# Edge keys from products on 64 rows of the array, picked keys added by VectorE, and 3 picked tiles in 16 in place of 4

## The reference

```python
Q = (nodes @ wq + bq).reshape(n, H, DK)
K = (nodes @ wk + bk).reshape(n, H, DK)
V = (nodes @ wv + bv).reshape(n, H, DK)
scores = (Q[row] * K[col]).sum(-1) * inv_sqrt_dk
ef = (edge_attr @ we + be).reshape(-1, H, DK)      # edge_attr: 200000 x 64, we: 64 x 128
scores = scores + (Q[row] * ef).sum(-1) * inv_sqrt_dk
es = jnp.exp(scores)
denom = jax.ops.segment_sum(es, row, num_segments=n)
msg = (es / (denom[row] + 1e-08))[..., None] * V[col]
out = jax.ops.segment_sum(msg, row, num_segments=n).reshape(n, -1) @ wo + bo
```

## Time and profile before

| | |
|---|---|
| median of 3 runs (lowest to highest) | 4399.89 us (4384.28 to 4402.94) |
| the profiled execution, its time | 4383.41 us |
| its span | 4381.6 us |
| mean granted clock of TensorE | 0.96 of full speed |
| TensorE busy | 87% of the span |
| GpSimd busy | 66% |
| VectorE busy | 61% |
| ScalarE busy | 39% |

### The profile page before, as it was taken

The page is one execution under the profiler, slowest core; times in us unless marked ns, Lnnn a source line. Parts: engine busy times, 40 slices in busy tenths (PEclk is TensorE's granted clock), DMA queues, the critical chain, the costliest instruction groups (busy, mean ns, idle before and its releaser), DMA issues.

```text
span 4381.6 us, 91625 instructions
## 1 busy us (share of the span) xinstructions
PE 3832.3 (87%) x24957; PEld 2675.4 (61%) x24958; DVE 2673.1 (61%) x5858; ACT 1730.6 (39%) x4596; POOL 2880.5 (66%) x2878
## 2 busy tenths in 40 slices
PE   5557877369999999999995899999999999999994
PEld 3234444134454544545443688888888888888883
DVE  8999999231131311313115677777777777777777
ACT  0046666130010100101003566666666666666662
POOL 3167887777777777777776466666666666666660
PEclk8989999679999999999997999999999999999997
DMA  9525555479999899998993566666666666666661
GB/s 374 212 93 186 186 192 179 167 239 356 332 325 356 299 356 333 320 356 302 355 348 117 159 173 173 173 174 173 174 174 173 174 173 174 173 174 173 174 174 52
DMA packets 507359, 982.36 MB, mean 224 GB/s; under 512 B 280679, under 2 KB 298035, under 8 KB 505384
## 3 DMA queue, kind: packets, MB, share of 16 engines
q1 hardware_dynamic: 362280, 656.78, 45.9%
q0 software_dynamic: 113856, 229.87, 16.9%
q10 hardware_dynamic: 31168, 95.09, 6.5%
HBM read 781.05 MB, written 200.41 MB: 224 GB/s over the span
## 4 chain that ended last, share of the span: by engine, by line
PE 42%; POOL 37%; issue 12%; DVE 2%; ACT 1%; DMA 1%; DVEq 0%; SPq 0%; POOLq 0%; ACTq 0%
POOL records L1032 36%; PE ps L1805 10%; PE ps L1823 9%; PE ps L1809 8%; PE ps L1798 5%; PE ps L1815 4%; PE ps L1778 2%; PE ps L1776 2%; PE ps L1787 1%; PE ps L1438 1%; POOL recs L1014 0%; POOL recs L1015 0%; ACT deg L1481 0%; DVE deg L2141 0%; DVE st_f L2127 0%
## 5 line engine op out<-in xcount | busy, mean ns | idle before, releaser
L1032 POOL DMA_INDIRECT records<-recs,pos x1562 | 1619.9, 1037 | 478.9 <-issue 470.7
L1744 POOL DMA_INDIRECT kv<-kv_table,rec x1213 | 1168.3, 963 | 747.2 <-DVE msg L1989 423.0
L1154 PE MATMUL ps<-adj,mh 128*128 128x500 f16 (+1 forms) x6370 | 1309.0, 366 | 6.4 <-DVE mh L1305 5.6
L1154 PEld LDWEIGHTS ps<-adj,mh 128*128 128x128 f16 x6370 | 619.3, 97 | 675.1 <-issue 7.7
L1326 DVE TENSOR_TENSOR adj<-adj,quarter 128x128 f16<-128x128 f16 (+25 forms) x305 | 46.2, 210 | 766.1 <-DMA adj<-adj_full 758.2
L1809 PE MATMUL ps<-we,at 128*128 128x256 f32 x1616 | 483.0, 381 | 0.0
L1192 ACT ACTIVATE sc<-sc 128x1 f32<-128x1 f32 x6 | 1.2, 203 | 1216.0 <-DVE sc L1274 973.3
L1805 PE MATMUL ps<-qn,oht 128*128 x3232 | 457.1, 285 | 5.2 <-ACT at L1872 1.2
L1823 PE MATMUL ps<-msg,ohf 128*128 128x136 f32 x3232 | 443.0, 280 | 4.9 <-DVE msg L1989 4.9
L1805 PEld LDWEIGHTS ps<-qn,oht 128*128 128x128 f32 x3232 | 392.3, 191 | 75.9 <-issue 75.9
L866 ACT ACTIVATE blk<-ps 128x490 f16<-128x490 f32 x625 | 335.1, 587 | 226.9 <-PE ps L795 225.9
(11 more groups left out here) (325 smaller groups left out, 5378.0 us busy)
## 6 DMA issues: line engine op xcount, KB each, us to landing
adj<-adj_full SPq DMA_DIRECT2D x420, 875.0 KB, 6.0
x1t<-kv_table SPq DMA_DIRECT2D x404, 256.0 KB
adj_full<-blk SPq DMA_DIRECT2D x12, 6125.0 KB
records<-deg ACTq DMA_DIRECT2D x1, 56576.0 KB, 170.5
rec<-records SPq DMA_DIRECT2D x404, 136.0 KB
records<-recs,pos POOLq DMA_INDIRECT x1562
recs<-in_edge_attr ACTq DMA_DIRECT2D x18, 1344.0 KB, 13.2
kv<-kv_table,rec POOLq DMA_INDIRECT x1213
```

The lines of the kernel that those rows point to most:

```text
L1032: G.indirect_dma_start(out=k.rec_d, out_offset=bass.IndirectOffsetOnAxis(ap=k.pos[:, at:at + 1], axis=0), in_=k.recs[:, q, j, :], in_offse ...
L1154: last = mm(bank, mh[:, part, hi, :], adj[:, c, x * width:(x + 1) * width], start=(hi == 0 and part == 0), stop=True, skip_group_check=True)
L1744: G.indirect_dma_start(out=kv[:, q, j, :], out_offset=None, in_=k.kv_d, in_offset=bass.IndirectOffsetOnAxis(ap=rec[:, q, j, RD:RD + 1].bit ...
```

## The change

Four things are edited.

- The edge keys are made by four products instead of two: each takes the 64 rows of `at` of one tile and 64 rows of `we`, and 128 columns. Rows 0 to 63 serve the even tiles and rows 64 to 127 the odd ones. Queries and edge keys of a group now share two banks: even tiles in one (queries in columns 0 to 255, edge keys in the rest), odd tiles in the other (edge keys first).
- ScalarE's `lift_keys` is gone. VectorE adds the picked keys straight from PSUM: its addition runs over all four tiles, with `kv` of tile 0 set to zero once (`memset`), and no longer waits for ScalarE.
- The scaling by 0 or 1 is put into the exponential of tile 0 (`goodscale`), which becomes a ScalarE instruction of its own in groups with a pick.
- `PICKS` has three entries instead of four: groups with `q` = 3 gather all four tiles and have no window, no `spot` and no picked keys or values.

```diff
-PICKS = (0, 1, 2, 3)
+PICKS = (0, 1, 2)
...
+        def query_at(s, j):
+            return PS[:, 2 + 2 * s + j % 2, (2 * (j % 2) + j // 2) * P:(2 * (j % 2) + j // 2 + 1) * P]
+
+        def edge_at(s, j):
+            return PS[:, 2 + 2 * s + j % 2, (2 - 2 * (j % 2) + j // 2) * P:(2 - 2 * (j % 2) + j // 2 + 1) * P]
...
                 for j in range(GT):
-                    mm(PS[:, 2 + q % S, j * P:(j + 1) * P], oht[:, q % S, j, :],
+                    mm(query_at(q % S, j), oht[:, q % S, j, :],
                        k.qn[:, bass.ds(b[j // 2], 1), :].rearrange("p a c -> p (a c)"), start=True, stop=True)
                 pick = q in PICKS
-                for j in range(0, GT, 2):
-                    last = mm(PS[:, 4 + q % S, j * P:(j + 2) * P], at[:, q % S, j // 2, :], we[:, :, :].rearrange("p j d -> p (j d)"),
-                              start=True, stop=not (pick and j == 0), skip_group_check=True)
-                    if pick and j == 0:
+                for j in range(GT):
+                    half = slice(j % 2 * F, (j % 2 + 1) * F)
+                    last = mm(edge_at(q % S, j), at[half, q % S, j // 2, :], we[half, j % 2, :], start=True, stop=not (pick and j == 0),
+                              skip_group_check=True)
+                    if pick and j == 1:
                         x = PICKS.index(q)
                         pe.wait_ge(wl[x], 16 * i + 16)
                         for h in range(2):
-                            mm(PS[:, 4 + q % S, 0:P], spot_t[:, q % S, h, :], window[:, x, h, 0:D], start=False, stop=(h == 1), skip_group_check=True)
+                            mm(edge_at(q % S, 0), spot_t[:, q % S, h, :], window[:, x, h, 0:D], start=False, stop=(h == 1), skip_group_check=True)
...
-            def lift_keys(g, q, i):
-                if q not in PICKS:
-                    return
-                done(act, "queried", g)
-                before(act, "scored", g, S)
-                act.sem_inc(sem("rec_gated"), 1)
-                A.activation(kq[:, q % S, 0, :], PS[:, 4 + q % S, 0:D], ACT.Identity, scale=goodcol[:, bass.ds(g, 1)]).then_inc(lifted, 1)
...
-                A.activation(msg[:, q, :, D:MW], sc[:, q % S, :].rearrange("p (j h) -> p j h", h=HEADS), ACT.Exp,
-                             scale=DK ** -0.5).then_inc(S_["weighed"], 1)
-            steps(act, ENG.Activation, ((lift_keys, 2), (pack, 0), (evacuate, 1), (weigh, 2), (lift_values, 2)))
+                j = GT - gathered(q)
+                scores = sc[:, q % S, :].rearrange("p (j h) -> p j h", h=HEADS)
+                last = A.activation(msg[:, q, j:GT, D:MW], scores[:, j:GT, :], ACT.Exp, scale=DK ** -0.5)
+                if j:
+                    last = A.activation(msg[:, q, 0, D:MW], scores[:, 0, :], ACT.Exp, scale=goodscale[:, bass.ds(g, 1)])
+                last.then_inc(S_["weighed"], 1)
+            steps(act, ENG.Activation, ((pack, 0), (evacuate, 1), (weigh, 2), (lift_values, 2)))
...
+            for q in PICKS:
+                V.memset(kv[:, q, 0, 0:D], 0.0)
...
-                j = GT - gathered(q)
-                if j:
-                    v.wait_ge(lifted, i * (2 * NPICK) + (2 * (PICKS.index(q) + NPICK) + 1))
-                ch.link(V.tensor_tensor(kq[:, q % S, j:GT, :], kv[:, q, j:GT, 0:D], PS[:, 4 + q % S, j * P:].rearrange("p (j c) -> p j c", c=D), ALU.add))
-                ch.link(V.tensor_tensor(kq[:, q % S, :, :], kq[:, q % S, :, :], PS[:, 2 + q % S, :].rearrange("p (j c) -> p j c", c=D), ALU.mult))
+                ch.link(V.tensor_tensor(by_half(kq[:, q % S, :, :]), by_half(kv[:, q, :, 0:D]), edges_of(q % S), ALU.add))
+                ch.link(V.tensor_tensor(by_half(kq[:, q % S, :, :]), by_half(kq[:, q % S, :, :]), queries_of(q % S), ALU.mult))
```

More of the change, by code:

```diff
@@ L1595, in attend, with queries_of, edges_of, by_half @@
         basecol = of(k.x1t, NG).bitcast(I32)
-        goodcol, badcol = of(k.x1t, NG), of(k.x1t, NG)
+        goodcol, badcol, goodscale = of(k.x1t, NG), of(k.x1t, NG), of(k.x1t, NG)
+        def query_at(s, j):
+            return PS[:, 2 + 2 * s + j % 2, (2 * (j % 2) + j // 2) * P:(2 * (j % 2) + j // 2 + 1) * P]
+        def edge_at(s, j):
+            return PS[:, 2 + 2 * s + j % 2, (2 - 2 * (j % 2) + j // 2) * P:(2 - 2 * (j % 2) + j // 2 + 1) * P]
+        def queries_of(s):
+            both = PS[:, 2 + 2 * s:4 + 2 * s, :].rearrange("p b c -> p (b c)")
+            return both.rearrange("p (x c d) -> p x c d", c=2, d=D)[:, 0:4:3, :, :]
+        def edges_of(s):
+            both = PS[:, 2 + 2 * s:4 + 2 * s, :].rearrange("p b c -> p (b c)")
+            return both[:, 2 * P:6 * P].rearrange("p (o c d) -> p o c d", c=2, d=D)
+        def by_half(of_):
+            return of_.rearrange("p (c o) d -> p o c d", o=2)
         given[0] = 0
@@ L1613, in attend @@
         wl = [sem(f"rows_loaded{q}") for q in range(len(PICKS))]
-        spotted, picked, lifted = sem("spots_turned"), sem("values_picked"), sem("keys_and_values_lifted")
+        spotted, picked, lifted = sem("spots_turned"), sem("values_picked"), sem("picked_values_lifted")
         NPICK, NONE = len(PICKS), 65536.0
@@ L1786, in round_spots @@
                 for h in range(2):
-                    last = nc.tensor.transpose(PS[:, 4 + q % S, h * (P // 2):(h + 1) * (P // 2)].bitcast(BF16),
+                    last = nc.tensor.transpose(edge_at(q % S, 1)[:, h * (P // 2):(h + 1) * (P // 2)].bitcast(BF16),
                                                spot[:, PICKS.index(q), h * P:(h + 1) * P], identb[:, :])
@@ L1852, in act_att @@
                 act.sem_inc(S_[n], AHEAD)
-            act.sem_inc(lifted, 2 * NPICK)
+            act.sem_inc(lifted, NPICK)
             def pack(g, q, i):
@@ L1870, in evacuate @@
                         act.wait_ge(picked, i * NPICK + (PICKS.index(x) + 1 + (1 - back) * NPICK))
-                    A.activation(spot_t[:, q % S, :, :].rearrange("p h c -> p (h c)"), PS[:, 4 + q % S, 0:P].bitcast(BF16), ACT.Copy)
+                    A.activation(spot_t[:, q % S, :, :].rearrange("p h c -> p (h c)"), edge_at(q % S, 1).bitcast(BF16), ACT.Copy)
                 A.activation(at[:, q % S, :, :].rearrange("p j c -> p (j c)"), T_AT[q % S], ACT.Copy).then_inc(S_["evacuated"], 1)
@@ L1950, in dve_att @@
             V.tensor_copy(goodcol, PS[:, 1, 0:NG])
+            V.tensor_scalar(goodscale, PS[:, 1, 0:NG], DK ** -0.5, None, ALU.mult)
             V.tensor_scalar(badcol, PS[:, 1, 0:NG], -1.0, 1.0, ALU.mult, ALU.add).then_inc(table_ready, 1)
@@ L1994, in message @@
                 if q in PICKS:
-                    v.wait_ge(lifted, i * (2 * NPICK) + (2 * (PICKS.index(q) + NPICK) + 2))
+                    v.wait_ge(lifted, i * NPICK + (PICKS.index(q) + 1 + NPICK))
                 weighted(q, slice(0, GT)).then_inc(S_["messages"], 1)
```

## The result

The changed kernel takes 4274.14 us, the median of 4 runs (4263.17 to 4284.92); the kernel before, on the same chip, 4392.99 us, the median of 4 (4384.28 to 4402.94). The ratio is 0.9732, with a 95% interval of 0.9699 to 0.9765. It is faster, inside the range, but by 119 us where 171 had been forecast (4392.99 against 4222). The profiled execution took 4284.92 us. The times of both kernels lie on two levels some 20 us apart (4384 to 4386 and 4400 to 4403; 4263 to 4264 and 4284 to 4285), so a smaller difference of medians says little by itself, and the length of the edge attention, read from the traces, is the better measure.

What follows compares the result with a forecast made beforehand. TensorE was taken to bound the edge attention, in a circle of waits with ScalarE. Its pass, 18.34 - 0.84 - 1.05 + 0.1 = 16.55, plus 0.1, gave 16.65 us: 169 us gained, median 4222 us, range 4180 to 4330.

Steps and rivals of the forecast that it cites:

- The circle: Edge attention: TensorE and ScalarE wait for each other through the key lift; removing it returns 3 x 0.28 = 0.84 us a pass.
- turn of the loop: Loop end in edge attention: stops all engines, adds 0.80 us to VectorE's pass; no change in TensorE's turn was forecast.
- One pick fewer: TensorE, group with q = 3: no picked keys, spots or picked values, saving 1.05 us a pass.
- The edge keys: TensorE's eight 128-column instructions run one behind the other, +0.1 us a pass; complete overlap would give -1.8.
- Both rivals: TensorE's edge products: array emptied at each 64/128-row change (slower, chance 0.17), or halves overlapping (4180 to 4200 us, chance 0.22).
- the first rival: TensorE's array empties at each 64/128-row change: 0.17 us each, 14 a pass, some 4440 us; chance 0.17.
- VectorE: Edge attention: addition over four tiles costs 687 instead of 554 ns; VectorE's pass becomes 16.5 us, an upper value.
- GpSimd: Edge attention gathers: thirteen a pass instead of twelve at 1.26 us each, 16.4 us a pass.
- reserve: GpSimd's idle time of about 1 us a group waiting for `msg`, said to pay for the thirteenth gather.
- Interlock: Edge attention: TensorE, VectorE and GpSimd fit closely at 16.4 to 16.6 us, so 0.1 us a pass was added.
- my forecast itself: Edge products run one behind the other, pass 16.5 to 16.9 us, so 4200 to 4250 us; chance 0.40.
- interlocked engines: Rival for the edge attention: the slower engine of each step counts, pass 17.3 us, 4285 us; chance 0.15.

Runs made afterwards that it cites:

- lift_only_b: Kernel before with only ScalarE's lift of the picked keys removed (VectorE adds them from PSUM), four picks and old edge products kept: 4269.39 us, ratio 0.9732.
- picks_only_b: Kernel before with three entries in PICKS instead of four and nothing else changed: 4263.10 us, ratio 0.9716.
- full_rows_b: Changed kernel with each edge product on all 128 rows instead of 64: 4246.69 us, ratio 0.9677; on a chip with standstills (full_rows) ratio 1.0174.
- window_last_b: Changed kernel, edge products in tile order 2, 3, 0, 1 and picked-key products behind all four, one 64-row block a group: 4239.15 us, ratio 0.9668.

## Why the prediction was right in its sign and too large in its gain

**The circle: right.** The gap from `att` to queries is 0.22 us in every step, VectorE's wait for the lift is gone, and lift_only_b shows the dense step at 4.20. The term was -0.84 a pass; alone it gave 18.34 - 17.22 = 1.12, the rest being the shorter turn of the loop (0.59 to 0.28), which I had left as it was.

**One pick fewer: right.** The term was -1.05; picks_only_b measured 18.34 - 17.07 = 1.27, in which one of the three waits of the circle, 0.28, is counted as well.

**The edge keys: this step failed.** Two smaller terms failed beside it, the pauses of GpSimd and the turn of the loop, both below. The step said: "I take +0.1, because each of these instructions brings its own weights and no row here shows two loads of weights at once." Both rivals that I had set against this were true at once. The halves overlap, and completely (the bound that I had put at -1.8), and each change between 64 and 128 rows costs what the first rival had worked out. The chances treated them as cases that exclude one another; they are two terms of one sum. By the rows of the changed kernel a group with a picked tile pays 0.10 on the queries, 0.20 in each block and 0.20 on the picked keys, and about 0.02 on the spots behind: 0.72 for four changes, 0.18 each. The other group pays 0.10 + 0.21 + 0.01 = 0.32 for two. The four groups together pay 3 x 0.72 + 0.32 = 2.48, and the overlap returns 4 x 0.44 = 1.76. What stands there is **+0.7 a pass, not +0.1**. With it the sum for TensorE is 18.34 - 0.84 - 1.05 + 0.72 = 17.17, and 17.08 was measured.

The Trainium skill (TensorEngine Tiling (Array Packing), Tiling Modes, Key Properties) says that changing the tiling mode drains the engine, and that different tiles load weights and multiply in parallel. The traces agree with both, in 0.16 to 0.21 us for a change (0.32 to 0.42 for the pair into a block and out of it) and in 1.09 against 0.65 us for eight instructions on one half or on two. The rival had worked out 0.17 from the difference between an instruction's length, 0.28, and its spacing, 0.11, and 14 changes at 0.17 are 2.4 us a pass against 2.48 by the rows.

The weights aren't loaded ahead across a change either, and the rival had said that this would come on top; the 0.16 to 0.21 hold both. The first load of the block (engine PEld) starts when its first product does, 3303.78, while within a mode it starts earlier (that of L1822 at 3302.68 for products from 3302.79):

```profile
3302.68 0.97 PEld L1822 LDWEIGHTS ps<-qn,oht 128*128 128x128 f32 x8
3303.78 0.30 PEld L1827 LDWEIGHTS ps<-we,at 64*128 64x128 f32 x4
```

**VectorE: as computed.** The addition takes 685 ns, where 687 had been taken.

**GpSimd: right on average, wrong on what it leaves.** Thirteen gathers at 1.26 are 16.4 us, less than TensorE's pass. But once in every 104 gathers, which is every eighth pass, GpSimd idles for 0.9 to 2.5 us instead of 0.30. One of the twelve such places of the changed kernel, in the timelines of GpSimd and of VectorE:

```profile
3019.80 0.95 POOL L1761 DMA_INDIRECT kv<-kv_table,rec  x1 [2.21 <-issue]
...
3028.07 0.69 DVE L1995 TENSOR_TENSOR kq<-kv,ps 128x512 f32<-128x512 f32 x1 [1.88 <-DMA kv<-kv_table,rec]
```

VectorE waits 1.88 us for that gather's group, the one with four gathers. The twelve passes that hold such a pause last 17.5 to 18.8 us, against the median of 17.08. The kernel before had the same idles, 1.2 to 1.3 us once in 105 gathers, where their neighbours have 0.30; this is one of them:

```profile
2609.12 1.12 POOL L1744 DMA_INDIRECT kv<-kv_table,rec  x1 [1.30 <-issue]
```

There they vanished in the 1 us that GpSimd waited for `msg` in each group: no pass of its loop is more than 0.4 us above the median. I had called this wait a reserve that "pays for the thirteenth gather and is then gone", without asking what else it had been paying for. These pauses are a term that the sum did not have. They lift the mean of the pass 0.10 above its median in the changed kernel, and 0.24 and 0.25 in full_rows_b and window_last_b, where the other engines leave less room.

**Interlock and the turn of the loop: the wrong term.** I had added 0.1 for the interlock to TensorE's 16.55 and left the turn of the loop at its old length. The interlock is hardly there: from 3200 to 4200 us TensorE's sums wait for `msg` three times, 4.6 us in all. The turn does move, by TensorE's own load of block numbers. Where the last instructions ahead of it become cheaper, part of the gain goes into waiting for that load. In the changed kernel it stays by luck about what it was (0.55 against 0.59), since the dear edge products fill the time. In full_rows_b, whose TensorE is the one of the prediction, it grows by 0.25: 18.34 - 0.84 - 1.05 + 0.02 + 0.25 = 16.72, and 16.75 was measured.

So gains do not add. Breaking the circle gave 1.12 and one pick fewer 1.27, each alone; both together gave 18.34 - 16.75 = 1.59, not 2.39. Of the 0.80 between them 0.28 is the wait that both remove; most of the rest is the turn, 0.31 shorter than before in lift_only_b and 0.25 longer in full_rows_b.

**The account.** Forecast pass 16.65, measured mean 17.18: 0.53 x 100 = 53 us, and 4274 - 4222 = 52. By the sum, 0.10 of the 0.53 are the idles of GpSimd, and 0.43 the edge products (0.62 more than taken, less the 0.1 for the interlock and 0.09 that the measured pass lies below TensorE's sum). By experiment the edge products count for less. With them as the prediction took them, full_rows_b still has a mean pass of 16.99, 0.34 above the forecast: 0.24 for the idles of GpSimd, and 0.10 because the turn takes 0.25 where 0.1 had been set aside. Undoing the halves alone gives back 0.19. The two ways differ because the terms stand in for one another.

**What was luck.** The time lies in the range, but above the 4200 to 4250 of my forecast itself. It comes nearer to the 4285 that I had given to interlocked engines, and the upper end of the range, 4330, was set by that case; the mechanism behind it is not the one that the runs show.

**What stays open.** What makes GpSimd idle every 104 gathers wasn't tried. No run moves the load at the turn of the loop. And which of the two faster versions is better rests on one profiled execution of each: by the ratios, one block of halves a group (0.9668) and none (0.9677) are alike, by stage and pass the first is ahead. Both are faster than the changed kernel as a pass, 16.59 and 16.75 against 17.08.

## What to carry to other kernels

Two mechanisms that act on the same instructions (halves run side by side; each change between 64 and 128 rows costs time) are to be added up, not weighed as alternatives: count the instructions that the overlap saves and the changes that it takes, and put them so that one block holds as many as there are. Four instructions on two halves saved 0.22 us and cost about 0.36 for two changes here; eight saved 0.44 and cost 0.32 to 0.42, so even a block of eight brought hardly anything: 0.05 us a group with a pick (2.18 against 2.23) and 0.14 without. When the work ahead of a loop's turn gets shorter, ask what the engine's own queue does there: a load of 1.94 us there took back 0.25 us a pass in full_rows_b. And before an engine's idle time is spent on new work, look in its timeline for rare long pauses that the idle time now hides.

## What the runs showed of the hardware

- A change between 64-row and 128-row products costs 0.16 to 0.21 us, half of what the pair into a block and out of it costs, in three places: the products ahead (0.99 for 0.89), the block (0.20 on top of 0.11 an instruction), the products behind (0.55 for 0.44, or 0.64 between two blocks).
- The first weights behind such a change are loaded as their product starts (0.00 us ahead); elsewhere the load starts 0.11 us ahead of it.
- The halves overlap wholly in both orders of the block that ran: 0.65 us alternating in pairs, 0.65 with four and four, 1.09 on one half alone.
- At the turn of the loop TensorE's queue takes 2.6 to 2.7 us from the branch to the next product, 1.94 of them for loading block numbers; with 16 matmul instructions yet to start at the branch the engine idles 0.28 to 0.84 us.
- GpSimd pauses once in 104 indirect gathers for 0.9 to 2.5 us in the changed kernel, and once in 105 for 1.2 to 1.3 in the one before.
- A chip on which the same kernel takes 6840 us instead of 4390, with standstills and a mean clock of 0.80 instead of 0.96, also turned the order of variants around: full_rows was slower than before there by 1.7% and faster by 3.2% elsewhere.
